# Attended rows and sums of weights moved by DMA into rows by feature, and divided per batch

## What is computed

```python
q, k, v = split_heads(x @ Wq.T), split_heads(x @ Wk.T), split_heads(x @ Wv.T)   # 16 heads of 8
q, k = _rope(q, pos), _rope(k, pos)
score = jnp.where(causal, einsum('bqd,bkd->bqk', q, k), -inf)
attn = softmax(score / sqrt(8), axis=-1)
out = einsum('bqk,bkd->bqd', attn, v)        # attended rows
return out.reshape(b, s, 128) @ Wo.T
```

## Time and profile before

| what | value |
|---|---|
| runs | 800.43, 800.54 (median), 805.24 us |
| the profiled execution | 801.62 us; span from its first to its last instruction 799.6 us |
| TensorE, matmuls | 751.4 us busy, 94% |
| VectorE | 609.3 us, 76% |
| ScalarE | 506.8 us, 63% |
| GpSimd | 313.9 us, 39% |
| DMA | 51.84 MB, mean 65 GB/s |

### The profile page before, as it was taken

One profiled execution on the slowest core, in us unless ns is written; L12 is line 12 of the kernel. 1 busy time (PEld: TensorE's weight loads), 2 busy tenths in 40 slices (PEclk: granted clock), 3 DMA queues, 4 the chain that ended last, 5 costly groups with the idle time before them and its releaser, 6 DMA issues. The chain is left out here.

```text
span 799.6 us, 17942 instructions
## 1 busy us (share of the span) xinstructions
PE 751.4 (94%) x5618; PEld 438.9 (55%) x5618; DVE 609.3 (76%) x1919; ACT 506.8 (63%) x1229; POOL 313.9 (39%) x603
## 2 busy tenths in 40 slices
PE   9899999888999999999999999999999978699994
PEld 8888997455434344434433443334344337688994
DVE  5757774499999898889889888988898508746663
ACT  2156662486267787778777877787787762156662
POOL 6077744176423223322422342233223310175753
PEclk8599999999999999999999999999999999689998
DMA  8822212127642133123303321332130000321110
GB/s 261 312 54 52 57 36 93 45 80 184 159 75 37 27 60 62 28 35 61 58 16 51 62 44 20 62 60 37 27 61 4 2 6 31 119 56 40 52 39 27
DMA packets 27989, 51.84 MB, mean 65 GB/s; under 512 B 7552, under 2 KB 19200, under 8 KB 26496
## 3 DMA queue, kind: packets, MB, share of 16 engines
q1 hardware_dynamic: 21296, 41.04, 22.1%
q0 software_dynamic: 4096, 8.69, 4.2%
q10 hardware_dynamic: 2512, 1.06, 0.5%
HBM read 35.40 MB, written 14.97 MB: 63 GB/s over the span
## 5 line engine op out<-in xcount | busy, mean ns | idle before, releaser
L1411 DVE CUSTOM_DVE_ANT_0 cst<-psS,mask_row 128x768 bf16<-128x768 f32 (+7 forms) x512 | 362.1, 756 | 41.5 <-PE psS L1284 37.4
L1374 ACT ACTIVATE prob<-psST 128x512 f32<-128x512 f32 (+3 forms) x750 | 320.2, 498 | 107.9 <-PE psST L1316 86.9
L1331 PE MATMUL a_psO<-prob,vs 128*32 128x512 f32 (+3 forms) x1536 | 157.5, 496 | 0.4 <-ACT p_anT L1380 0.2
L1482 POOL TENSOR_TENSOR a_gate<-a_zeros 1x1 f32<-1x1 f32 x128 | 23.4, 183 | 290.7 <-ACT prob L1374 290.5
L1316 PE MATMUL psST<-a_qs,ks 75*128 75x512 bf16 (+1 forms) x480 | 125.8, 328 | 0.0
L1284 PE MATMUL psS<-ks,a_qs 72*128 72x512 bf16 (+2 forms) x480 | 112.4, 326 | 0.1
L777 POOL DMA_INDIRECT tok<-rows,f_there_number x64 | 61.7, 964 | 86.4 <-DVE f_number L489 42.6
L1316 PEld LDWEIGHTS psST<-a_qs,ks 75*128 75x128 bf16 x480 | 42.7, 97 | 80.5 <-ACT prob L1374 50.4
L1483 POOL TENSOR_SCALAR_AFFINE_SELECT prob<-prob 128x512 f32<-128x512 f32 x128 | 79.9, 624 | 0.0
L1316 PE MATMUL psST<-qs,ks 75*128 75x512 bf16 (+3 forms) x270 | 71.8, 328 | 0.1
L1284 PE MATMUL psS<-ks,qs 72*128 72x512 bf16 (+3 forms) x288 | 67.8, 327 | 0.6 <-DVE a_rowmax L1411 0.3
(11 more groups left out here) (185 smaller groups left out, 1080.4 us busy)
## 6 DMA issues: line engine op xcount, KB each, us to landing
a_qs<-q_split SPq DMA_DIRECT2D x60, 96.0 KB
rows<-tok SPq DMA_DIRECT2D x8, 536.0 KB, 5.1
ks<-k_split SPq DMA_DIRECT2D x32, 128.0 KB
qs<-q_split SPq DMA_DIRECT2D x36, 96.0 KB
q_split<-p_part SPq DMA_DIRECT2D x24, 128.0 KB, 2.4
k_split<-p_part SPq DMA_DIRECT2D x24, 128.0 KB, 2.4
ks<-k_split SPq DMA_DIRECT2D x16, 192.0 KB
tok<-x_after_first SPq DMA_DIRECT2D x4, 536.0 KB, 5.2
```

Source lines behind the costliest of these rows:

```text
L1331: last = nc.tensor.matmul(psO[32 * h:32 * h + 32, c0:c0 + w], vs[r][:, j, h, :], prob[:, u % RING, h, 0:w], start=(j == 0), stop=(u + 1 in ...
L1374: nc.scalar.activation(prob[:, u % RING, h, 0:w], score_buffer(s, u * QH + h)[:, 0:w], ACT.Exp, scale=SCALE).then_inc(exp_done, 1)
L1411: last = nc.vector.tensor_tensor_reduce(out=out[:, a * CH:a * CH + width], in0=ps[:, a * CH:a * CH + width], in1=mask_row[:, S - width:], ...
```

## The change

The values get 8 columns of ones in place of one, so `psO` holds each head's sums eight times, in the 8 rows behind its 8 attended rows. `turn_out`, `normalise`, the letters A and B and, in the second feed-forward, `turn` of `shared` with ScalarE's copies are gone. For each stage and half SyncE issues 8 DMAs (`keep`): for each head its 8 rows of sums into `weight_sums[ch]` and its 8 attended rows into `shared`, which is now by feature (128 features x 4096 tokens). When the four stages of a batch are in, VectorE takes the reciprocal of a whole `weight_sums[ch]` of 128 x 512 in place (`invert`), and GpSimd multiplies it into `shared` (`divide`). `outT` has two buffers. The three strings are new.

```diff
+            n.kept, n.inverted, n.divided = [sem(f"kept{i}") for i in range(NCH)], sem("inverted"), sem("divided")
...
-        link(nc.gpsimd.memset(n.vs[r][:, :, :, DK + 1:], 0.0))
-        link(nc.gpsimd.memset(n.vs[r][:, :, :, DK:DK + 1], 1.0))
+        link(nc.gpsimd.memset(n.vs[r][:, :, :, 2 * DK:], 0.0))
+        link(nc.gpsimd.memset(n.vs[r][:, :, :, DK:2 * DK], 1.0))
...
+            if r == 1:
+                invert(dve, n, B - 1, 1)
             statistics()
...
             def project(g):
-                u = turn_of[True, g]
-                pe.wait_ge(turned_copied, u + 1)
+                pe.wait_ge(n.divided, g + 1)
                 wait(pe, added, g - 1)
...
             else:
-                turn(True, 0)
-                turn(True, 1)
                 for g in range(G):
                     project(g)
-                    if g + 2 < G:
-                        turn(True, g + 2)
...
             if r == 0:
                 first_block_pool(nc, pool, n)
+            else:
+                divide(pool, n, B - 1, 1)
...
+def invert(dve, n, b, ch):
+
+    dve.wait_ge(n.kept[ch], 2 * QH * 16 * (b + 1) * (H // QH))
+    dve.reciprocal(n.weight_sums[ch], n.weight_sums[ch]).then_inc(n.inverted, 1)
...
+def divide(pool, n, b, ch):
+
+    pool.wait_ge(n.inverted, b * NCH + ch + 1)
+    rows = n.shared[:, b * TB + ch * CB:b * TB + (ch + 1) * CB, :].rearrange("p n d -> p (n d)")
+    pool.tensor_tensor(rows, rows, n.weight_sums[ch], ALU.mult).then_inc(n.divided, 1)
...
-    MIDDLE = ("sstswtstsstswssNtstswstsstswwsstssBstsstwstsstsstwssttsswtssAsststwssMsttsswssttssswwsts")
...
+    MIDDLE = ("sstswtstwtsstssNwsssttsswssstssstwsststswtsstsstwsssttsswtsstsstwsMststsswsststsswwsts")
...
+    COPIES = {FIRST: (5, None), MIDDLE: (6, 1), LAST: (6, 1)}
+
+    INVERT_AFTER = (4, 5)
...
+        def keep(s, ch):
+
+            sp.wait_ge(out_copied, 2 * s + ch + 1)
+            if s % QB == 0:
+                wait(sp, n.divided, (s // QB - 1) * NCH + ch + 1)
+            for h in range(QH):
+                rows = slice(s % QB * RW + h * DK, s % QB * RW + (h + 1) * DK)
+                sp.dma_start(weight_sums[ch][rows, :],
+                             outT[ch][32 * h + DK:32 * h + 2 * DK, :]).then_inc(n.kept[ch], 16)
+                sp.dma_start(attended[rows, ds(s // QB * S + ch * CH, CH)],
+                             outT[ch][32 * h:32 * h + DK, :]).then_inc(n.kept[ch], 16)
 
         def stage(s):
             if s > 0:
                 load_max(s, s % RING, 1)
             if s > 0 and s + 2 < NST:
                 load(s + 2, (s + 2) % RING)
+            if s > 0:
+                keep(s - 1, 1)
+            keep(s, 0)
             if s + 1 < NST:
                 load_max(s + 1, (s + 1) % RING, 0)
...
         run(stage)
+        keep(NST - 1, 1)
...
             act.wait_ge(pv_done, s * UN + half_end[ch])
-            wait(act, out_read, 2 * s + ch)
-            nc.scalar.activation(outT[:, :], psO[:, :], ACT.Copy).then_inc(out_copied, 1)
+            wait(act, n.kept[ch], KEPT * s)
+            nc.scalar.activation(outT[ch][:, :], psO[:, :], ACT.Copy).then_inc(out_copied, 1)
...
-                else:
-                    normalise(of, arg, k, psS[k % 2])
+                if s % QB == 0 and s > 0 and what == "tile" and arg in INVERT_AFTER:
+                    invert(dve, n, s // QB - 1, INVERT_AFTER.index(arg))
 
         run(stage)
+        invert(dve, n, B - 1, 0)
...
                     split(s + 1, 0)
                     values(s + 1, (s + 1) % RING)
+                    if s % QB == 0 and s > 0:
+                        for ch in range(NCH):
+                            divide(pool, n, s // QB - 1, ch)
                 mask(s, u)
...
         run(stage)
+        divide(pool, n, B - 1, 0)
```

More of the change, by code:

```diff
@@ L337, in ffn @@
                              "h_high", "y_done", "y_biased", "gated", "y_ready"))
-        turns = [(n.tok, g, logits_done, CB * (g + 1)) for g in range(G)]
-        if r == 1:
-            turns = [(n.shared, g, multiplied, g + 1) for g in range(G)]
+        turns = [(g, logits_done, CB * (g + 1)) for g in range(G if r == 0 else 0)]
         WIDE = D + E
@@ L344, in ffn @@
                     for i in range(2)]
-        turn_of = {(source is n.shared, g): u for u, (source, g, _, _) in enumerate(turns)}
         def item(i):
@@ L570, in _, with turn @@
         def _(pe):
-            def turn(after, g):
-                u = turn_of[after, g]
-                wait(pe, turned_copied, u - 1)
+            def turn(g):
+                wait(pe, turned_copied, g - 1)
                 for j in range(CB):
-                    last = nc.tensor.transpose(wide_ps[u % 2][:, j * P:(j + 1) * P],
-                                               (n.shared if after else n.tok)[:, g * CB + j, 0:D], n.c("ident"))
+                    last = nc.tensor.transpose(wide_ps[g % 2][:, j * P:(j + 1) * P], n.tok[:, g * CB + j, 0:D],
+                                               n.c("ident"))
                 last.then_inc(turned, 1)
             def project(g):
-                u = turn_of[True, g]
-                pe.wait_ge(turned_copied, u + 1)
+                pe.wait_ge(n.divided, g + 1)
                 wait(pe, added, g - 1)
                 for j in range(CB):
-                    last = nc.tensor.matmul(attended[g % 2][j // 2][:, j % 2, :], xT[u % XT][:, j * P:(j + 1) * P],
+                    last = nc.tensor.matmul(attended[g % 2][j // 2][:, j % 2, :], n.shared[:, g * CB + j, :],
                                             n.out_and_router, start=True, stop=True)
@@ L602, in _ @@
                     pe.wait_ge(n.x_loaded[g // NCH], 16)
-                    turn(False, g)
+                    turn(g)
                     if g == 1:
@@ L702, in _ @@
                 if u >= XT:
-                    _, _, read, count = turns[u - XT]
+                    _, read, count = turns[u - XT]
                     act.wait_ge(read, count)
@@ L862, in project @@
     anT = [sb(f"anT{i}", [P, CH]) for i in range(2)]
-    n.outT = anT[0]
+    n.outT, n.weight_sums = anT, [an[i][:, :, :].rearrange("p n d -> p (n d)") for i in range(2)]
     rot, tmp, rest = ([[n.prob[:, m, 2 * i + k, :] for k in range(2)] for i in range(2)] for m in range(3))
@@ L1168, in attention @@
     program = [jobs(s) for s in range(NST)]
-    program[-1].append(("turn_out", NST - 1, 1, 0))
-    uses = [[(what, of, arg) for what, of, arg, _ in found if what in ("tile", "turn_max", "turn_out")]
+    uses = [[(what, of, arg) for what, of, arg, _ in found if what in ("tile", "turn_max")]
             for found in program]
@@ L1210, in attention @@
     outT = n.outT
-    recip = [n.mean[:, i * CB * QH:(i + 1) * CB * QH].rearrange("p (b h) -> p b h", b=CB) for i in range(NCH)]
     psO = psum("psO", CH)
@@ L1214, in attention @@
     QB = H // QH
+    attended, weight_sums, KEPT = n.shared[:, :, :].rearrange("p n d -> p (n d)"), n.weight_sums, 2 * QH * 16
     (cleared, v_ready, scored, use_done, use_read, exp_done, masked, pv_done, out_copied, split_done,
-     maxT_ready, split_chain, out_read) = (sem(k) for k in (
+     maxT_ready, split_chain) = (sem(k) for k in (
          "cleared", "v_ready", "scored", "use_done", "use_read", "exp_done", "masked", "pv_done",
-         "out_copied", "split_done", "maxT_ready", "split_chain", "out_read"))
+         "out_copied", "split_done", "maxT_ready", "split_chain"))
     stack_loaded = [n.first_stack_loaded] + [sem(f"stack_loaded{i}") for i in range(1, RING)]
@@ L1292, in turn_max @@
             nc.tensor.transpose(ps[:, 0:P // 2].bitcast(BF16), maxparts[:, :], n.identb[:, :]).then_inc(use_done, 1)
-        def turn_out(s, ch, index, ps):
-            use(index)
-            pe.wait_ge(out_copied, 2 * s + ch + 1)
-            for b in range(CB):
-                last = nc.tensor.transpose(ps[:, b * P:(b + 1) * P], outT[:, b * P:(b + 1) * P], n.c("ident"))
-            last.then_inc(use_done, 1)
         def score(s, u, h):
@@ L1353, in stage @@
                     turn_max(of, arg, k, ps)
-                else:
-                    turn_out(of, arg, k, ps)
                 k += 1
```

27 lines of the change are left out of this document (6 added, 21 removed).

## The result

The changed kernel takes 866.76 us (865.44 to 868.68, 4 runs), the kernel before on the same chip 801.83 us (800.43 to 805.24, 4 runs): a ratio of 1.080, 95% interval 1.077 to 1.083. The direction was as forecast; the size was not: 838 us had been predicted, and the time lies 15 us above the range. The ratios leave out a run that lies over 1.5% above the fastest of its kernel, in which the granted clock was lower; that is one run in all, of 868.60 us, of the kernel with work for TensorE during the wait.

The account below looks back on a forecast made before the run. TensorE's written order, with VectorE through two PSUM buffers, sets the pace; 801.6 - 16.0 (stages) + 53.1 (three boundaries) + 0.3 (tail) = 839.0, the runs' median 1.1 below that execution, so 838 us; range 806 to 852.

Parts of the forecast that it names:

- the first stall: Stages 4, 8, 12: TensorE stands 2.2 us while VectorE's first reciprocal delays the copy of maxima (0 to 4.5).
- TensorE's reach ahead: Second stall: TensorE's work before tile 8, which needs tile 6 read by VectorE, lasts 3.8 us.
- rival 1: Batch boundaries: transfers land before VectorE's second reciprocal, only the reciprocals cost; 797 us, chance 0.10.
- a cheap reciprocal (2): VectorE's reciprocal takes 0.68 us, first stall 0; 822 us, chance 0.22 together with stalls shorter than counted.
- an overtaking of the loads (3): Sums' transfers overtake the loads, landing 9.9 us after the copy of maxima, not 12.2; 831 us, within the forecast's 0.50.
- T: Zero point in stages 4, 8, 12: the end of VectorE's copy of maxima between tiles 4 and 5.
- The clock: Behind the second stall: TensorE runs 5 us at half pace, losing 2.5 us a boundary.
- The gain of a stage: Each of 14 middle stages, without two turns and two divisions, shrinks by 1.1 us (0.86 to 1.52).
- rival 4: Middle stages stay at 27.24 us, turns covered, new order losing elsewhere; 853 us, chance 0.12 together with dearer stalls.
- The landing: Boundaries: half 1's sums land behind the loads, 12.2 us after the copy of maxima (9.9 to 13.6).
- The tail: After the last copy, before the second block's first sum: issues and a reciprocal cost +0.3 us (-2 to +3).
- The first stage: First attention stage loses one turn: 0.55 us shorter.

Follow-up runs that it names:

- The filler: Changed kernel plus 56 matmuls of 512 columns on TensorE ahead of tile 8 in stages 4, 8 and 12: 851.61 us, ratio 1.060.
- the sums ahead: Changed kernel with SyncE's 8 DMAs of the half before issued ahead of the 11 loads, not behind them: 853.06 us, ratio 1.062.
- The last two kernels: Changed kernel, sums ahead of loads, second sums buffer, reciprocals in pieces: behind tiles 2, 6, 10, 14, 808.71 us (1.008); in VectorE's idle gaps, 793.45 us (0.990).

## Why the prediction was wrong

**What held.** VectorE's in-order wait as the cause; where it stands; the reciprocal, 3.35 us for 3.26 forecast, 6.2 ns a column; the first stall, 2.21 for 2.2; TensorE's reach ahead, 4.1 us (339.93 to 344.05) for 3.8; GpSimd's multiplication, 1.26 us, below the bound of 1.46. Not slower (rival 1), a cheap reciprocal (2) and an overtaking of the loads (3) are excluded by the rows: the wait is 12.56 us, the reciprocal takes 3.35, and the wait for the sums ended at T + 13.8, not T + 9.9. By the repeat count that the Trainium skill gives ("VectorE: DVE Perf Modes", First, the fixed hardware budget) the prediction's estimate for a reciprocal was 4.27 us; the measurement decides.

**The clock, the term that failed: 2.5 forecast, 9.6, 6.0 and 6.0 measured** as what a boundary costs beyond a plain stage and its two stalls (52.64 - 26.60 - 16.45 = 9.59), 14 us of the 30 that the sum fell short. I read one restart, at the end of the first block, where the clock was back 5 us after work began again, and applied it to another kind of work. Behind these stalls TensorE was busy for 17.4, 11.7 and 11.3 us while the clock stayed at 1.2 GHz: half of that lost is 8.7, 5.9 and 5.7. With the reciprocals cut short the same account holds: 10.8, 8.1 and 8.1 beyond the stalls, for halves of 11.6, 8.4 and 8.5. At the first boundary the clock falls already behind the first stall (0.53 is its mean from 341.00 to 352.00), which I had not counted; at the other two it falls in the second stall, as it does with the reciprocals cut short, where there is no first. The filler shows the clock as the cause of at least 17.3 of the 21.6 us, 5.8 a boundary; the rest is not shown. Why the same stage came back after 17 us once and after 11 twice no run here tells.

**The gain of a stage: 1.1 forecast, 0.70 measured**, 5.6 us in 14 stages. I assumed that a stage shrinks by at least what TensorE loses. The old letters without turns show that it shrinks by 0.1: rival 4's heading was right, the turns were covered, and its reason was not: the new order, which it had losing and I had at zero, gains 0.6. Of my two errors the one made up for half of the other; that the measured 0.70 lies as near to the forecast as it does is luck.

**The landing: T + 12.2 forecast, T + 13.8 measured** (13.3 and 14.2 at the other two), which is nearly all of the 5.2 us by which the stalls are longer (50.8 in all, for 45.6). The engines' work ended about when I said (share 0.05 in the window that begins at 352.00, T + 12.1). But the wait ends 1.6 us behind that (1.3 and 1.6 at the other two), and I had called a transfer landed when the engines fell silent. The Trainium skill ("DMA: Bandwidth & Descriptors", Anatomy of one DMA) puts a fixed cost of about 2 us on a transfer, most of it the receipt of the write; its table is for another issuing engine, but the 1.6 here, and 1.4 from the last issue's end to the wait's end with the sums ahead, are of that size; what the time is spent on no run here shows. The issue of 0.62 us, twice what I took, was not what this boundary waited for, as the sums read from the chip's memory show.

**The tail: +0.3 forecast, +1.8 from stage 15's M to the first sum.** There the issues count in full: the last copy of attended rows ends at 720.04, the eighth issue at 725.35, VectorE's last reciprocal starts at 726.73 and the first sum at 730.00, 10.0 us behind the copy, where before it was 8.4. The first stage, forecast 0.55 shorter, is 0.8 longer; which of its letters costs that was not tried. The rows of the tail, on ScalarE and VectorE:

```profile
719.44 0.60 ACT L1393 ACTIVATE p_anT<-a_psO 128x512 f32<-128x512 f32 x1 [1.48 <-PE a_psO L1346]
...
726.73 3.35 DVE L1095 RECIPROCAL p_an<-p_an 128x512 f32<-128x512 f32 x1 [8.12 <-DMA shared<-p_anT]
...
730.00 0.11 DVE L387 TENSOR_TENSOR f_logit<-early,f_ps_half 128x16 f32<-128x16 f32 x1
```

**Added up.** The profiled execution took 868.7 us, 29.7 above the sum's 839.0: 14.1 beyond the stalls, 5.6 in the plain stages, 5.2 in the stalls, 1.5 in the tail, 1.3 in the first stage, and 2.0 outside of what was changed.

**The slack of VectorE.** I wrote that VectorE's 3 us of slack could not repay the stalls. The last two kernels sharpen that: the slack lies at fixed places. Outside them 3.8 us of VectorE's work cost 2.57; inside them up to 1.9 cost less than 0.1 (26.67 us for 26.62).

## What to carry to other kernels

Before a wait is put into an engine's order, find where its data lands, counting from the semaphore and not from the end of the transfer, and put the wait behind that; then cut the work to the size of the idle gaps that the engine's timeline shows, for the sum of its idle time says little. A stall of TensorE costs what follows it too: price the clock by several restarts under the same kind of work, and take as a bound that the rest of the stage runs at half pace, as it nearly did here at the first boundary. A busy engine that loses work need not give it back: here removing two turns gave 0.1 us a stage and a new order of the same jobs 0.6.

## What the runs showed of the hardware that was not expected

- TensorE's clock stayed at 1.2 GHz for 11.3 to 17.4 us of work behind a stall of 14 to 15 us, and for 16.8 to 23.2 behind one of 12 with the reciprocals cut short; at the first block's end it was back after 5. At one boundary it fell within 2 us of the end of a stall of 2.2 us, while TensorE worked.
- SyncE took 0.625 us in the median to issue a DMA of 16 KB (8 rows of 512 numbers) whose source is on the core, 0.46 in the median for the same shape from the chip's memory.
- From the DMA engines' last bytes to the release of the wait it took 1.3 to 1.6 us at the three boundaries.
- Two changes of function on ScalarE, to Ln and back to Exp, cost two table loads of 1.28 us each, twice the operations; a power on GpSimd took 81.9 us for 128 x 512 numbers, where its multiplication takes 1.26.
